# Quantised graph layer: whole numbers as int16 written by ScalarE and transposed as bits, clamps on VectorE, weights on GpSimd, another group order

## What is computed

```python
h = max(layernorm(x), 0)
# first layer, 4-bit activations, 3-bit weights
xq  = round(min(h / act_alpha, 1) * 15)
wq  = round(clip((w - mean(w)) / std(w) / wgt_alpha, -1, 1) * 7)      # signed
s   = relu(xq @ wq * scales)                                          # 2048 x 512
sq  = round(min(s / act_alpha2, 1) * 15)
x1  = x + (adj @ sq) * scales
# second layer
g   = max(layernorm(x1), 0)
A   = dinv * ((adj + adj.T) / 2 + I) * dinv       # dinv from the row sums
out = x1 + (adj @ (1e-8 * A)) @ g                 # as y = Coefficient2 @ A @ g with Coefficient2 = adj
```

## Time and profile before

| | us |
|---|---|
| median of 3 runs | 529.84 (528.91 to 529.9) |
| profiled execution | 530.4, of which the span is 528.6 |
| TensorE busy | 501.2 |
| VectorE busy | 294.6 |
| ScalarE busy | 161.6 |
| GpSimd busy | 1.1 |

### The profile page before, as it was taken

One profiled execution on the slowest core, in us unless ns is written; L12 is line 12 of the kernel. 1 busy time (PEld: TensorE's weight loads), 2 busy tenths in 40 slices (PEclk: granted clock), 3 DMA queues, 4 the chain that ended last, 5 costly groups with the idle time before them and its releaser, 6 DMA issues.

```text
span 528.6 us, 6538 instructions
## 1 busy us (share of the span) xinstructions
PE 501.2 (95%) x2472; PEld 247.9 (47%) x2472; DVE 294.6 (56%) x417; ACT 161.6 (31%) x218; POOL 1.1 (0%) x8
## 2 busy tenths in 40 slices
PE   1577999999999999999999999999999999999997
PEld 1543565655555444444444444444444444444443
DVE  3976488899997888887789687823100100010000
ACT  1578595545463415344461212122000000000000
POOL 0000000000000000000000000000000000000000
PEclk9879999999999999999999999999999999999999
DMA  6980050353545403323232323106300010000001
GB/s 233 400 321 0 2 179 21 106 178 128 175 136 175 135 5 119 120 80 119 85 111 83 119 88 110 40 1 238 121 20 20 20 40 20 20 35 25 20 20 40
DMA packets 19250, 51.63 MB, mean 98 GB/s; under 512 B 2336, under 2 KB 2336, under 8 KB 19232
## 3 DMA queue, kind: packets, MB, share of 16 engines
q1 hardware_dynamic: 18656, 51.39, 28.4%
q10 hardware_dynamic: 576, 0.00, 0.1%
HBM read 42.99 MB, written 8.39 MB: 97 GB/s over the span
## 4 chain that ended last, share of the span: by engine, by line
PE 88%; DVE 7%; DMA 2%; ACT 2%; issue 1%; SPq 0%; ACTq 0%
PE ps_a L911 31%; PE ps_p L812 18%; PE ps_p L874 7%; PE ps_a L874 7%; PE ps_b L874 7%; PE ps_h L874 3%; PE ps_m L874 3%; PE ps_a L799 2%; PE ps_b L799 2%; DMA feat<-in_x 2%; PE ps_h L812 1%; PE ps_m L812 1%; DVE st L478 1%; DVE small L685 1%; ACT at L342 1%
## 5 line engine op out<-in xcount | busy, mean ns | idle before, releaser
L812 PE MATMUL ps_p<-small,at 128*128 128x512 f16 x448 | 102.4, 379 | 0.0
L753 DVE SCALAR_TENSOR_TENSOR feat<-ps_a,feat 128x512 f32<-128x512 f32 x16 | 11.1, 692 | 153.8 <-PE ps_a L911 153.8
L911 PE MATMUL ps_a<-small,at 128*128 128x512 f16 x384 | 85.5, 379 | 0.0
L911 PE MATMUL ps_a<-a_in,at 128*128 128x512 f16 x384 | 85.5, 379 | 0.0
L812 PEld LDWEIGHTS ps_p<-small,at 128*128 128x128 f16 x448 | 43.7, 98 | 45.4
L385 ACT ACTIVATE split<-a_in 128x1024 f16<-128x1024 f32 x30 | 31.7, 1056 | 101.9 <-PE ps_p L874 90.0
L911 PEld LDWEIGHTS ps_a<-small,at 128*128 (+1 forms) x384 | 37.6, 98 | 45.3
L911 PEld LDWEIGHTS ps_a<-a_in,at 128*128 (+1 forms) x384 | 37.6, 98 | 45.3
L681 DVE TENSOR_TENSOR split<-a_in,split 128x1024 f16<-128x1024 f32 x30 | 36.7, 1224 | 34.0 <-ACT split L385 34.0
L874 PE MATMUL ps_p<-feat,split 128*128 (+1 forms) x180 | 43.9, 379 | 0.5 <-DVE small L685 0.5
L874 PE MATMUL ps_a<-feat,split 128*128 (+1 forms) x180 | 43.7, 379 | 0.0
(11 more groups left out here) (147 smaller groups left out, 444.0 us busy)
## 6 DMA issues: line engine op xcount, KB each, us to landing
a_in<-in_adj SPq DMA_DIRECT2D x54, 512.0 KB, 3.7
out<-feat SPq DMA_DIRECT2D x32, 256.0 KB, 2.0
feat<-in_x SPq DMA_DIRECT2D x8, 512.0 KB, 11.3
at<-in_adj SPq DMA_DIRECT2D x8, 512.0 KB, 14.6
feat<-out SPq DMA_DIRECT2D x4, 1024.0 KB, 9.4
at<-in_L_gnn_weight SPq DMA_DIRECT2D x2, 512.0 KB, 5.5
split<-in_adj SPq DMA_DIRECT2D x1, 512.0 KB, 16.3
tmp<-in_adj SPq DMA_DIRECT2D x1, 512.0 KB, 17.0
```

The costliest lines, as they stand in the source:

```text
L753: nc.vector.scalar_tensor_tensor(xr, BANK[t % 2], 1.0 / (SA * SZ), xr, ALU.mult, ALU.add)\
L812: last = nc.tensor.matmul(l0_bank(r), at_block(r, lo, j), small[:, j * D:(j + 1) * D], start=(j == 0 and lo == 0), stop=(j == T - 1 and lo ...
L911: last = nc.tensor.matmul(BANK[n], at_block(t, lo, j), z_part(j, z_lo), start=(j == 0 and lo + z_lo == 0), stop=(j == T - 1 and lo == 1))
```

## The change

- ScalarE's normalisation writes int16 into `xq` (seen as float16 by the transpose): a positive scale, relu, no 15 added (so one small operation less in each `group_scale`). `quantise` and its buffer `hq` go; the transposes read `xq` and wait for `xn_ready`.
- What the transposes left in PSUM is read as int16 by VectorE, which clamps to 15 and writes `hT` as float16 (`clamp_rows`); `copy_transposes` goes.
- `scale_support` writes int16; one VectorE operation (`clamp_support`) clamps and converts in place of two.
- The weights are scaled by GpSimd into int16 and clamped by one VectorE operation for each half (`clamp_weights`).
- `GROUPS` has six groups in place of five, with 2, 2, 2, 4, 2 and 4 tiles. The three queues of the first stage get a new order; `support(m)` now follows its own `transpose_rows(m)`, where one pair's transposes lay between before, and `support(0)` comes ahead of `transpose_rows(1)`.

```diff
-GROUPS = (0, 2, 4, 8, 12, T)
+GROUPS = (0, 2, 4, 6, 10, 12, T)
...
+            def scale_weights(h):
+
+                pool.wait_ge(c_wgt_ready, 1)
+                nc.gpsimd.tensor_scalar(w_num[:, 2 * h * D:2 * (h + 1) * D].bitcast(i16),
+                                        w_raw[:, 2 * h * D:2 * (h + 1) * D], c_wgt, b_wgt, ALU.mult, ALU.add)\
+                  .then_inc(w_scaled, 1)
+
+            scale_weights(0)
+            scale_weights(1)
...
                 if n >= 2:
-                    act.wait_ge(hq_ready, n - 1)
+                    act.wait_ge(hT_ps, n - 1)
                 for t in (2 * n, 2 * n + 1):
-                    last = nc.scalar.activation(xq[n % 2][:, (t % 2) * D:(t % 2 + 1) * D], feat[:, t * D:(t + 1) * D],
+                    last = nc.scalar.activation(xq[n % 2][:, (t % 2) * D:(t % 2 + 1) * D].bitcast(i16),
+                                                feat[:, t * D:(t + 1) * D],
                                                 ACT.Relu, bias=shift[:, t:t + 1], scale=rd[:, t:t + 1])
                 last.then_inc(xn_ready, 1)
...
             def scale_support(m):
                 act.wait_ge(sup_ps, m + 1)
                 if m >= 2:
-                    act.wait_ge(sup_rounded, m - 1)
-                nc.scalar.activation(sq[m % 2], sup_banks(m)[:, :], ACT.Relu, scale=c_sup).then_inc(sup_out, 1)
-
-            def scale_weights(h):
-                act.wait_ge(c_wgt_ready, 1)
-                half = w_raw[:, 2 * h * D:2 * (h + 1) * D]
-                nc.scalar.activation(half, half, ACT.Identity, bias=b_wgt, scale=c_wgt).then_inc(w_scaled, 1)
+                    act.wait_ge(sq_ready, m - 1)
+                nc.scalar.activation(sq[m % 2].bitcast(i16), sup_banks(m)[:, :], ACT.Relu, scale=c_sup)\
+                  .then_inc(sup_out, 1)
...
             group_root(0)
             normalise(0)
-            scale_weights(0)
             group_root(1)
-            scale_weights(1)
             normalise(1)
-            copy_transposes(0)
+            scale_support(0)
             group_root(2)
-            copy_transposes(1)
+            hi_turned(0)
             normalise(2)
-            scale_support(0)
-            hi_turned(0)
-            normalise(3)
-            copy_transposes(2)
-            group_root(3)
             scale_support(1)
             hi_turned(1)
-            copy_transposes(3)
-            for n in range(4, T // 2):
-                if n == 5:
-                    group_root(4)
-                normalise(n)
-                scale_support(n - 2)
-                copy_transposes(n)
-            scale_support(T // 2 - 2)
-            scale_support(T // 2 - 1)
+            group_root(3)
+            normalise(3)
+            scale_support(2)
+            normalise(4)
+            group_root(4)
+            scale_support(3)
+            normalise(5)
+            scale_support(4)
+            group_root(5)
+            normalise(6)
+            scale_support(5)
+            normalise(7)
+            scale_support(6)
+            scale_support(7)
...
-                link(nc.vector.scalar_tensor_tensor(shift[:, a:b], mv3[:, a:b, 0], -1.0, rd[:, a:b],
-                                                    ALU.mult, ALU.mult), fill[5])
-                nc.vector.tensor_scalar(shift[:, a:b], shift[:, a:b], float(ACT_LEVELS), None, ALU.add)\
-                  .then_inc(shift_ready, 1)
-
-            def quantise(n):
-
-                dve.wait_ge(xn_ready, n + 1)
-                if n >= 2:
-                    dve.wait_ge(hT_ps, n - 1)
-                nc.vector.tensor_scalar(hq[n % 2], xq[n % 2], -(MAGIC + ACT_LEVELS), MAGIC, ALU.add, ALU.add)\
-                  .then_inc(hq_ready, 1)
-
-            def round_support(m):
+                nc.vector.scalar_tensor_tensor(shift[:, a:b], mv3[:, a:b, 0], -1.0, rd[:, a:b],
+                                               ALU.mult, ALU.mult).then_inc(shift_ready, 1)
+
+            def clamp_rows(m):
+
+                dve.wait_ge(hT_ps, m + 1)
+                if m >= 2:
+                    dve.wait_ge(sup_ps, m - 1)
+                nc.vector.tensor_scalar(hT[m % 2], hT_ps_bank[m % 2].bitcast(i16), float(ACT_LEVELS), None, ALU.min)\
+                  .then_inc(hT_ready, 1)
+
+            def clamp_support(m):
                 dve.wait_ge(sup_out, m + 1)
-                nc.vector.tensor_scalar(small[:, 2 * m * D:2 * (m + 1) * D], sq[m % 2], MAGIC, -MAGIC,
-                                        ALU.add, ALU.add).then_inc(sup_rounded, 1)
-
-            def clip_support(m):
-                dve.wait_ge(sup_rounded, m + 1)
-                both = small[:, 2 * m * D:2 * (m + 1) * D]
-                nc.vector.tensor_scalar(both, both, float(ACT_LEVELS), None, ALU.min).then_inc(sq_ready, 1)
-
-            def round_weights(h):
+                nc.vector.tensor_scalar(small[:, 2 * m * D:2 * (m + 1) * D], sq[m % 2].bitcast(i16), float(ACT_LEVELS),
+                                        None, ALU.min).then_inc(sq_ready, 1)
+
+            def clamp_weights(h):
                 dve.wait_ge(w_scaled, h + 1)
-                return nc.vector.tensor_scalar(w_int[:, 2 * h * D:2 * (h + 1) * D], w_raw[:, 2 * h * D:2 * (h + 1) * D],
-                                               MAGIC, -MAGIC, ALU.add, ALU.add)
-
-            def weights_out(h):
-                half = w_int[:, 2 * h * D:2 * (h + 1) * D]
-                nc.vector.tensor_scalar(half, half, float(WGT_LEVELS), float(-WGT_LEVELS), ALU.min, ALU.max)\
-                  .then_inc(w_ready, 1)
+                nc.vector.tensor_scalar(w_int[:, 2 * h * D:2 * (h + 1) * D],
+                                        w_num[:, 2 * h * D:2 * (h + 1) * D].bitcast(i16),
+                                        float(WGT_LEVELS), float(-WGT_LEVELS), ALU.min, ALU.max).then_inc(w_ready, 1)
...
             bn(4)
-            quantise(0)
+            clamp_rows(0)
             group_scale(1)
-            link(round_weights(0), lambda: bn(5))
-            weights_out(0)
-            link(round_weights(1), lambda: bn(6))
-            weights_out(1)
+            clamp_weights(0)
+            clamp_weights(1)
+            link(bn(5))
             aggr(2)
-            link(bn(7))
-            aggr(3)
             group_var(GROUPS[2], GROUPS[3])
-            quantise(1)
-            group_scale(2, [lambda: bn(8), None, lambda: bn(9)])
-            aggr(4, lambda: bn(10))
+            clamp_rows(1)
+            bn(6)
+            group_scale(2)
+            link(bn(7), lambda: clamp_support(0))
+            aggr(3, lambda: bn(8))
+            lo_turned(0)
+            link(bn(9))
+            aggr(4)
+            group_var(GROUPS[3], GROUPS[4])
+            clamp_rows(2)
+            clamp_support(1)
+            bn(10)
+            group_scale(3)
+            lo_turned(1)
             link(bn(11))
             aggr(5)
-            group_var(GROUPS[3], GROUPS[4])
-            quantise(2)
-            round_support(0)
-            lo_turned(0)
-            group_scale(3, [lambda: clip_support(0), None, lambda: bn(12)])
-            quantise(3)
-            link(bn(13), lambda: round_support(1))
-            aggr(6, lambda: clip_support(1))
-            lo_turned(1)
-            bn(14)
+            group_var(GROUPS[4], GROUPS[5])
+            clamp_rows(3)
+            clamp_support(2)
+            bn(12)
+            group_scale(4)
+            bn(13)
+            link(bn(14), lambda: clamp_rows(4))
+            aggr(6, lambda: clamp_support(3))
             link(bn(15))
             aggr(7)
-            group_var(GROUPS[4], GROUPS[5])
-            quantise(4)
-            round_support(2)
-            group_scale(4, [lambda: clip_support(2)])
-            for n in range(5, T // 2):
-                quantise(n)
-                round_support(n - 2)
-                clip_support(n - 2)
-            for m in range(T // 2 - 2, T // 2):
-                round_support(m)
-                clip_support(m)
+            group_var(GROUPS[5], GROUPS[6])
+            clamp_rows(5)
+            group_scale(5)
+            clamp_support(4)
+            clamp_rows(6)
+            clamp_support(5)
+            clamp_rows(7)
+            clamp_support(6)
+            clamp_support(7)
...
-            keep_warm(14)
+            keep_warm(12)
             transpose_rows(0)
             keep_warm(4)
-            transpose_rows(1)
             pe.wait_ge(w_ready, 2)
             support(0)
+            keep_warm(2)
+            transpose_rows(1)
             turn(0)
-            transpose_rows(2)
             support(1)
             turn(1)
+            transpose_rows(2)
+            support(2)
             transpose_rows(3)
-            support(2)
+            layer0(0, [0, 1])
+            support(3)
             transpose_rows(4)
-            support(3)
+            layer0(0, [2, 3])
+            support(4)
             transpose_rows(5)
-            layer0(0, [0, 1])
-            support(4)
+            layer0(0, [4, 5])
```

(31 more changed lines are left out.)

## The result

The changed kernel takes 523.21 us (median; 522.98 to 524.94) against 529.73 for the kernel before: ratio 0.9887, 95% interval 0.9863 to 0.9911, so 6.0 us faster, between 4.7 and 7.3 (the means of the four executions each differ by 6.0, the medians by 6.5). Measured again later (see the second experiment) it took 523.37 against 529.47, ratio 0.9884 (0.9868 to 0.9901). The profiled execution, 524.94 with a span of 522.9, is the longest of the first four; part of what lengthens it is the subject of the second experiment.

What follows compares the result with a forecast made beforehand. TensorE bounds the kernel (busy 501.2 of 528.6 us), with 12.5 us idle between 12 and 54 us. 55.45 - 63.07 = -7.6 us, 3.4 from the clock and the rest idle time, gives 522.2 on the median; range 520.9 to 526.0.

Steps and rivals of the forecast that it cites:

- the walk: First-stage queues of four engines timed side by side: layer0(0, [12..15]) at 55.45 after, 63.64 before; error 0.57 us.
- the walk's mark: Start of layer0(0, [12..15]), forecast at 55.45 us against 63.07 in the trace before.
- The frame: Behind layer0(0, [12..15]) all shifts with TensorE, so the change is worth what it moves that start: -7.6 us.
- The unknown prices: First-stage operations without a matching row: clamp_rows 0.72, clamp_support and clamp_weights 0.41, GpSimd 1.5 us for each weight half.
- The step that failed: GpSimd's weight passes, 15.1 to 18.1 us, lie beside VectorE's statistics and group 1, whose shift ends at 19.3.
- rival C: VectorE and GpSimd hinder each other, delaying group_var(1): +1.3 to +2.9 us, 523.5 to 525.1; chance 0.2.
- Rival A: TensorE's clock falls again in a first-stage hole: +1.5 to +2.3 us, one stretch giving 523.7 to 524.5; chance 0.2.
- the early support alone: support(0) starts at 20.0 instead of 25.53: 5.5 us, half of it given back at turn(1).
- B: Slow int16 on VectorE: clamp_rows +3.7, other clamps +1.2, both +5.1 us; chance 0.1 first or both, 0.05 second with E.
- E: ScalarE writes int16 slower than float32 (0.94 a pass, 1.3 a support): 523.7 us; chance 0.05 with B's second.
- D: GpSimd's far longer passes delay support(0), eating the gain at 4.7 us each; chance 0.03 within 1 us, 0.04 slower.

Runs made afterwards that it cites:

- the second experiment: Changed kernel with 9 useless TensorE products before turn(1) and 6 before transpose_rows(3): 522.82 us, ratio 0.9885; changed kernel repeated as is: 523.37 us.

## Why the prediction was right

The forecast, 522.2, lies 1.0 us below the measured 523.21, inside the range; the prices and the walk along the queues were right, and two rivals that the forecast leaves out came in part. In the profiled execution it is less close: 522.8 forecast, 524.94 measured. From the walk's mark to the measured one it is 55.45, 55.53 (weights on ScalarE, full clock), 56.06 (GpSimd's passes, the clock held up), 57.40 (the clock low): of the 1.95 us between, 0.5 are GpSimd's and 1.3 come with the low clock.

- **The frame** held: the change was worth what it moved the start of `layer0(0, [12..15])`, 5.67 us in the profiled executions with 5.7 in the span, and 465.5 us follow it in every profile.
- **The walk** held to 0.1 us where its assumptions did: without GpSimd's passes and at full clock 55.53 against 55.45. Taking the absolute time and not the walk's difference to its own 63.64 was the right choice of the two. It is not as exact as that says: `scale_support` was under-sized by 0.09 (1.11, not 1.02) and the start 0.1 late, against `clamp_rows` at 0.69 and not 0.72.
- **From profile to median** there is an error of some 0.9 us that the walk does not have: the same run with the weights on ScalarE moves the mark by 7.5, but by its ratio it gains 6.7. The 63.07 that the 7.6 are counted from belongs to an execution with a span of 528.6; the later ones that the ratios use have spans of 526.5 to 528.0.
- **The unknown prices**: `clamp_rows` 0.69 (0.72), int16 clamps 0.42 (0.41): right. GpSimd 1.20 a pass (1.5): over-sized by a fifth. The estimate of 0.66 from the Trainium skill ("VectorE: DVE Perf Modes") is 0.03 off as well, on the other side.
- **The step that failed** is the one that left GpSimd's passes "beside VectorE's statistics and group 1". They hold up `group_var(1)` by 0.64 us and with it group 1. That was rival C, in size half of its +1.3, since the passes are shorter; it had one chance in five, and nothing in the rows spoke for or against it.
- **Rival A** had a chance of 0.2 and came in five of eight executions. Its place was right (behind the hole before `turn(1)`), its price was too high by the medians: 0.8 us between executions of one kernel, not 1.5 to 2.3, though 1.3 between two profiles. The row before it with the same idle time of 2.7 us deserved more weight than the busy stretch of 46 to 54.
- **Where I read the gain wrongly**: I wrote that the early support alone was 5.5 us, "half of it given back". The run with it alone shows 0.0. The gain is that of the new arithmetic, about two thirds of it the rows' part, in which TensorE's transposes no longer wait for a VectorE step and ScalarE loses `copy_transposes`; the new order adds nothing over the old one. So the forecast's size was right for this order, but its account of where the time comes from was not.
- **B and E** did not come: no slow int16 form, and ScalarE's int16 writes cost what its float32 ones do. Nor did D: GpSimd's pass is 1.20 us.

## What to carry to other kernels

Before an operation is given to GpSimd, list what VectorE runs in the same microseconds: here `tensor_scalar` from SBUF to SBUF, and operations with two SBUF inputs, waited inside their own duration, down to the smallest. When an engine's steps get shorter, check each queue for an awaited operation that stands behind one nobody waits for: three such moves in VectorE's queue brought 2 us here, where the new order had brought nothing. A wait of one engine hides another's low clock only if it comes behind it. Test "this is now earlier" by making it earlier alone. And when a profile is set against a median, look whether the profiled execution was a long one.

## What was not expected of the hardware

- Between int16 and float32 ScalarE's write type makes no difference here: 1.11 us for 128 x 1024 out of PSUM to either. The float16 form at 1.02 (L332 in the earlier trace rows) differs from both also in its scale, a constant and not one number per partition; that this is the reason is argued, not tried.
- A GpSimd pass of 128 x 1024 with two operations and a conversion to int16 takes 1.20 us beside VectorE's statistics and 1.22 on average over 30; the longest, 1.69, is the one that VectorE's small operations and `clamp_weights` ran ahead of.
- How long TensorE waits does not by itself tell whether its clock falls. Before the first support it stayed up after 2.61 us in the changed kernel and was down after 2.10 us in that with the second clamp; before `turn(1)` it stayed up with a wait of 2.68 us where ScalarE had the weights, and fell with one of 2.69 us in the changed kernel.
- Small whole numbers as int16 go through TensorE's float16 transpose in 0.61 us, as float16 numbers do (0.62), and the changed kernel's result rests on their bits coming out as they went in.
